# A decoder layer on one core: the weighing of the values in one run behind the next block's queries

## The reference, cut to what matters

```
for i in range(6):
    x = attn_layer(shift_tokens(x), Wqkv[i], q_scale[i], k_scale[i], Wo[i]) + x
    x = ffn_layer(shift_tokens(x), ln_g[i], ln_b[i], W1[i], b1[i], W2[i], b2[i]) + x

# attn_layer, 16 heads of 64, windows of 32 queries over 64 keys
q, k, v = split(x @ Wqkv)
q, k = l2norm(q) * qs, l2norm(k) * ksc
q = q * cos * scale + rotate_half(q) * sin * scale      # k with 1 / scale
sim = einsum('bhwie,bhwje->bhwij', q, k_of_two_windows) * 8     # masked
out = einsum('bhwij,bhwje->bhwie', softmax(sim), v_of_two_windows) @ Wo

# ffn_layer
xn = (x - mean) / sqrt(var + 1e-5) * g + b
a, gate = split(xn @ W1 + b1)
out = a * gelu(gate) @ W2 + b2
```

## Time and profile before

| | |
|---|---|
| median of 3 timed runs | 2067.36 us (2065.05 to 2070.86) |
| the profiled execution | 2071.8 us, of which the span from first to last instruction is 2070.0 us |
| TensorE busy | 1947.8 us, 94% of the span |
| VectorE, ScalarE, GpSimd busy | 1449.9 us, 1371.7 us, 1087.3 us |
| mean granted TensorE clock | 0.988; 1.00 in the stretches of the loop quoted below |
| DMA | 128.39 MB in 82214 packets |

### The profile page before, as it was taken

How to read it: one execution, slowest core, us unless ns; L and a number is a source line. 1 busy time by engine, 2 the same in 40 slices (tenths; PEclk the granted TensorE clock), 3 DMA queues, 4 the chain that set the end, 5 groups by cost and what they waited for, 6 DMA issues and landing times.

```text
span 2070.0 us, 75204 instructions
## 1 busy us (share of the span) xinstructions
PE 1947.8 (94%) x32520; PEld 1179.6 (57%) x32520; DVE 1449.9 (70%) x2239; ACT 1371.7 (66%) x2197; POOL 1087.3 (53%) x709
## 2 busy tenths in 40 slices
PE   8989897689999999999999999999999999999987
PEld 5655655355555555555555555565555555555553
DVE  1454545677787778777877777777777787778773
ACT  5565564466777667766776677767766777677763
POOL 1000000497666666666666666666666666666650
PEclk9999998799999999999999999999999999999998
DMA  3000001032223222232222323222332223222220
GB/s 118 2 1 1 2 21 31 22 83 64 63 64 94 74 74 63 64 94 74 73 64 65 82 75 81 74 65 75 85 80 73 65 62 95 74 74 63 64 64 21
DMA packets 82214, 128.39 MB, mean 62 GB/s; under 512 B 17247, under 2 KB 28125, under 8 KB 81885
## 3 DMA queue, kind: packets, MB, share of 16 engines
q1 hardware_dynamic: 81884, 123.59, 23.1%
HBM read 21.81 MB, written 1.05 MB: 11 GB/s over the span
## 4 chain that ended last, share of the span: by engine, by line
PE 73%; ACT 10%; DVE 10%; issue 6%; DMA 0%; ACTq 0%; SPq 0%; DVEq 0%
PE ps L619 13%; PE ps L623 13%; PE ps L645 9%; PE ps L704 7%; PE ps L696 6%; PE ps L689 6%; PE ps L429 4%; PE ps L669 3%; PE ps L628 3%; PE ps L632 2%; DVE work L1287 2%; DVE work L1106 2%; PE ps L525 2%; PE ps L443 1%; ACT work L1000 1%
## 5 line engine op out<-in xcount | busy, mean ns | idle before, releaser
L1457 POOL TENSOR_TENSOR work<-work,RS 128x1024 f32<-128x1024 f32 x192 | 365.6, 1904 | 385.8 <-ACT RS L971 384.7
L1101 DVE TENSOR_TENSOR work<-ps,work 128x512 f32<-128x512 f32 (+1 forms) x288 | 247.9, 861 | 265.7 <-ACT work L1032 228.6
L623 PEld LDWEIGHTS ps<-ident,work 128*128 128x128 f32 x3072 | 344.1, 141 | 118.6 <-issue 90.0
L623 PE MATMUL ps<-ident,work 128*128 128x128 f32 x3072 | 392.8, 275 | 14.6 <-ACT work L1000 11.2
L1476 POOL TENSOR_TENSOR work<-work 128x1024 f32<-128x1024 f32 x96 | 226.0, 2354 | 108.8 <-DVE work L1106 108.8
L1042 ACT ACTIVATE work<-work 128x1024 f32<-128x1024 f32 x96 | 101.6, 1058 | 268.3 <-DVE work L1216 268.3
L1468 POOL TENSOR_TENSOR work<-work 128x1024 f32<-128x1024 f32 x96 | 227.3, 2368 | 52.6 <-DVE work L1106 52.6
L1106 DVE TENSOR_TENSOR work<-ps,work 128x512 f32<-128x512 f32 (+1 forms) x288 | 247.4, 859 | 0.0
L1170 DVE TENSOR_REDUCE SS<-work 128x16 f32<-128x1024 f32 x192 | 231.6, 1206 | 0.0
L696 PEld LDWEIGHTS ps<-work 64*32 64x32 f32 x12288 | 135.0, 105 | 146.0 <-issue 133.3
L619 PE MATMUL ps<-WQ,XS 128*128 128x512 f32 x384 | 189.3, 616 | 8.0 <-issue 4.3
(11 more groups left out here) (185 smaller groups left out, 3094.0 us busy)
## 6 DMA issues: line engine op xcount, KB each, us to landing
work<-work SPq DMA_DIRECT2D x576, 128.0 KB
work<-work SPq DMA_DIRECT2D x336, 64.0 KB
WQ<-in_wqkv SPq DMA_DIRECT2D x6, 512.0 KB, 3.6
WK<-in_wqkv SPq DMA_DIRECT2D x6, 512.0 KB, 4.1
WV<-in_wqkv SPq DMA_DIRECT2D x6, 512.0 KB, 4.2
WO<-in_wo SPq DMA_DIRECT2D x6, 512.0 KB, 3.9
work<-ZR SPq DMA_DIRECT2D x48, 64.0 KB
W<-in_w SPq DMA_DIRECT2D x6, 341.0 KB, 3.5
```

The costliest lines, as they stand in the source:

```text
L623: m = nc.tensor.transpose(flat(R)[:, t * 128:t * 128 + 128], src[:, t * 128:t * 128 + 128], ident[:, :])
L1101: V.tensor_tensor(h16(cos_part[:, j, cols]), h16(src), rotary_tabs[:, at:at + 64].unsqueeze(1).broadcast_to([PARTS, heads_in, 64]), ALU.mu ...
L1457: U.tensor_tensor(h16(qk_norm[:, j, :]), h16(cos_part[:, j, :]), inv_norms[:, j, :].unsqueeze(2).broadcast_to([PARTS, 16, 64]), ALU.mult). ...
```

## The change

On TensorE, the weighing is issued as one run of 64 calls (128 matmuls) behind the next block's queries, instead of 32 calls before and 32 behind them; the queries get the wait for `probs_turned_copied`. In the steps with n = 0, `turn_tokens` moves from in front of the turning of the heads to behind it. On ScalarE, in the steps with n = 0, `inverse` moves ahead of the copy of the turned queries, and `invert_norms(g, 0)` moves behind the squares of the keys. The scores stay in two halves. VectorE, GpSimd and the DMA queue keep their order.

```
@@ TensorE, step @@
-                if f is not None and n == 0:
-                    turn_tokens(f)
                 if d:
                     pe.wait_ge(heads_copied, g - 2)
                     turn(bank_y, heads, 0, 4).then_inc(heads_turned, 1)
                     turn(bank_y, heads, 4, 8).then_inc(heads_turned, 1)
+                if f is not None and n == 0:
+                    turn_tokens(f)
...
-                if c:
-                    if a:
-                        pe.wait_ge(k_sin, 2 * g + 2)
-                    pe.wait_ge(probs_turned_copied, g - 1)
-                    pe.wait_ge(windows_loaded, 160 * (g - 1))
-                    weigh(0, 4)
                 if fo is not None and n == 2:
                     project_out(fo, 2, 3 if fo < FFN_PASSES - 1 else 8)
...
                 if g + 1 < ALL_BLOCKS:
                     if not b:
                         pe.wait_ge(q_sin, g + 1)
+                    if c:
+                        pe.wait_ge(probs_turned_copied, g - 1)
                     queries(g + 1)
                 if c:
-                    weigh(4, 8).then_inc(heads_weighed, 1)
+                    if a:
+                        pe.wait_ge(k_sin, 2 * g + 2)
+                    pe.wait_ge(probs_turned_copied, g - 1)
+                    pe.wait_ge(windows_loaded, 160 * (g - 1))
+                    weigh(0, 8).then_inc(heads_weighed, 1)
@@ ScalarE, step @@
+                if f is not None and n == 0:
+                    inverse(f)
                 if b:
                     act.wait_ge(q_turned, g)
                     A(q_t[:, :, :], turned(bank_z), ACT.Copy).then_inc(q_turned_copied, 1)
...
-                if f is not None and n == 0:
-                    inverse(f)
                 if f is not None and n == 1:
                     nc.scalar.preload_act_table_set(LNEXP)
+                late = f is not None and n == 0
+                if a and not late:
+                    invert_norms(g, 0)
                 if a:
-                    invert_norms(g, 0)
                     for half in range(2):
                         ...
                         A(squares[:, 1, 512 * half:512 * half + 512], bank_y[:, half, :], ACT.Square).then_inc(k_squared, 1)
+                if a and late:
+                    invert_norms(g, 0)
```

## The result

| | before | after |
|---|---|---|
| median | 2069.11 us (6 runs, 2065.05 to 2071.53) | 2054.63 us (6 runs, 2046.67 to 2058.2) |
| the profiled execution | 2071.8 us, span 2070.0 | 2056.84 us, span 2055.1 |

The changed kernel is faster: the ratio is 0.9925, with an interval of 0.991 to 0.9939. It gains 14.5 us. Forecast were 27.4 us and 2040; 2054.6 lies inside the range of 2024 to 2057, near its upper end.

What follows compares the result with a forecast made beforehand. VectorE's stream was taken to bound the key projection of n = 3 to L628 of n = 1, TensorE the rest. 13 + 8.4 + 1 + 3 + 2 = 27.4 us gave 2040 on the timed scale, range 2024 to 2057.

Steps and rivals of the forecast that it cites:

- Who bounds what: Loop pass: VectorE bounds from n = 3's key projection to n = 1's L628, TensorE elsewhere; pass 66.5 instead of 67.6 us.
- The rival that TensorE bounds throughout: Whole loop: all TensorE's waits and switches count, 41 us gained, 2026 us, a pass of 65.7; chance 0.09.
- `inverse` ahead of the copy: ScalarE, n = 0: VectorE's idle time before L1150 falls from 0.62 to at most 0.1 us; 13 us gained.
- The joined weighing: TensorE, weighing: one small-to-full switch fewer, 0.19 us a step, paying in n = 1 and 2; 8.4 us, bounds 0 and 10.6.
- The tokens behind the heads: TensorE, n = 0: ScalarE's heads copy up to 0.45 us sooner, 11.2 us of waits shrink to a fourth; worth 0.
- What is late next: TensorE: 0.5 to 0.8 us turn up as longer waits at L628 for gating, or partly L689 for the queries' copy.
- The supply of instructions: TensorE's instruction packets: 3 us gained in early steps, net 0 in the loop (-5 to +10), plus 2 from new slack.
- the early steps: TensorE, g = 2 to 5: the wait for VectorE's key products goes and pays only there, about 1 us.
- the gap stays: VectorE before L1150: it waits as before or another wait replaces the 0.62 us; 14 us gained, 2053; chance 0.13.
- Starvation: TensorE, end of the 128 matmuls: packets ending there cost up to 2.3 us each, 2095 us; chance 0.06.

Runs made afterwards that it cites:

- experiment 10: The changed kernel with never-waiting semaphore tests added on TensorE, making a loop pass 2560 instructions, ten packets: 2034.62 us, ratio 0.984 to the kernel before.
- experiment 2: The kernel before with ScalarE's two moves alone (`inverse` ahead of the queries' copy, query norms behind the key squares): 2065.78 us, ratio 0.9984.
- experiment 9: The kernel before with joined weighing and ScalarE's two moves, token transposes still ahead of the heads', padded to 2560 instructions a pass: 2036.99 us, ratio 0.9845.
- padded and joined: The kernel before with the joined weighing alone, padded with never-waiting tests to 2560 instructions a pass: 2043.92 us, ratio 0.9879 to the kernel before.
- experiment 7: The kernel before with only never-waiting semaphore tests added on TensorE, 2560 instructions a pass: 2062.06 us, ratio 0.9964 to the unpadded kernel before.
- experiment 4: The changed kernel with 43 never-waiting tests at the start and 42 a pass (2560 instructions), packet ends held at good places: 2039.4 us, ratio 0.986.
- experiment 5: The same padded changed kernel as experiment 4, with 128 more never-waiting tests at the start, moving packet ends half a packet: 2082.98 us, ratio 1.0071.

## Why the prediction was right and wrong

**Who bounds what: right.** Between the key projection of n = 3 and L628 of n = 1 VectorE's stream is the bound, elsewhere TensorE's. The shortest pass is 66.52 us against 66.5 forecast. With the packets held still (experiment 10) the passes are 66.2 and 66.6 in turn, 66.45 in the mean. The rival that TensorE bounds throughout would have had 65.7.

**`inverse` ahead of the copy: the mechanism right, the size half.** 13 us were counted, 6.9 were measured on top of the joined weighing and some 3 alone, there with more packet stalls than before. The gap did close as forecast, but the 13.9 us were read wrongly. The last of the 23 waits, at the end of the loop, is 3.57 us alone; it only shrinks to 2.7 in experiments 2 and 9. The 22 others are 10.3 us, and most are not 0.62 but 0.62 and 0.2 in turn. The pass before the one of the earlier trace rows has

```profile
1397.81 1.36 DVE L1150 TENSOR_SCALAR YC<-ps,YM,YQ 128x128 f32<-128x128 f32 x4 [0.19 <-ACT YQ L955]
```

And part of the gap is closed by the joined weighing too: the 22 waits are 9.1 us in the padded kernel before, and 5.8 padded and joined. The two terms overlapped and were added.

**The joined weighing: right place, half the size.** 8.4 us were counted, 0.19 a step in two steps of each pass. Measured are 0.17 (1.58 to 1.41) in the run and 0.19 in the queries, 0.36 a step; the steps' shortest times fell by 0.36 in n = 1, from 19.70 to 19.34, and by as much in n = 2 and 3. With 2 x 22 steps that is 15.8 us, and the early steps g = 2 to 8 give 2.8 more in the padded pair (93.9 to 91.1): 18.6, against 18.1 measured. (The median pass of the padded pair falls by 0.68, from 67.56 to 66.88, for twice 0.36.) The upper bound of 10.6 was too low, since it had only one side of the switch. The Trainium skill (TensorEngine Tiling (Array Packing), Key Properties) says that a change of tiling mode drains TensorE and gives no price; here going to small tiles and back costs 0.36 us.

**The tokens behind the heads: right.** It was counted at 0. The medians of the padded runs differ by 2.4 us, the undisturbed passes by 0.01. Its waits at L1000 went as forecast.

**What is late next: right.** L628 was to wait 12 us or more and waits 14.6 (26.4 with the packets still), and the copy of the queries costs 8.7 us at L689.

**The supply of instructions: this is the step that failed.** It counted a gain of 3 us in the early steps and 2 in the loop, +5. Without it the forecast was 22.4 us, and the work itself is worth 27.4 (experiments 7 and 10). What was measured is 14.5, so this term is -12.9 where +5 was counted. The gaps at packet boundaries, added up from the traces, put it at -10.9 in the loop (12.0 to 22.9), beyond the forecast's lower end of -5 there, and at +1.4 in the early steps (5.1 to 3.7), -9.5 together; the rest of the difference is not placed. Three things in it were wrong. It took the packet's least distance, 3.9 us, for a constant, whereas a packet that falls due while the window loads are issued starts up to 7.7 us after the boundary before instead of about 1.0, and the stall at 648.37 ends 9.3 us behind that boundary. It looked for the danger at the end of the long run of weighing, where the trace shows next to nothing (1.5 us at L696 in the whole run), while the stalls stand mostly in the second half of the scores, 14.3 of the 22.9 us in steps n = 0. And it counted ends by old stalls instead of by instruction number: 2518 to a pass and 256 to a packet would have told which passes are hit. That part of it which read the stalls as packets was right. By the rule of the Trainium skill (Runtime: NRT & Kernel Launch, Instruction fetch mechanics), by which the fetch is mostly hidden, the loops of experiments 4 and 5 should have agreed; their 21 passes are 24.8 us apart.

**The rivals.** The measured 2054.6 is next to the 2053 of "the gap stays", and it would be wrong to read it so: the gap went (1.0 us in one wait). Equal times do not show equal causes; the waits do. Starvation came, but elsewhere, and at 12.9 us it took nearly half of the gain and did not turn the result. That the padded kernels give 27.4 us, the very sum that was forecast, is chance: ScalarE's moves gave 6.9 for 13, the joined weighing 18.1 for 8.4 and the 1 us of the early steps, and the 5 of the supply were not in it. That 2054.6 lies in the range owes as much to these errors, which partly cancel, as to the mechanism.

What stays open: why a packet starts late while loads are issued, and how much of that is the number of loads; and how the joined weighing closes part of VectorE's gap.

## What to carry to other kernels

When TensorE stands in the middle of a run of equal matmuls with no semaphore behind it, count its instructions: if the stalls agree modulo 256, the time lost belongs to the place and not to the edit, and two orders can only be compared after padding both so that a loop pass is a multiple of 256. Put the padding where the engine waits anyway, and count its own price: here 0.108 us an instruction where nothing covers it. Count a switch between small and full matmuls on both sides, and do not add up two terms that close the same gap.

## What was not expected of the hardware

- The phase of the packets alone moves the loop's 21 passes from 1404.4 to 1429.2 us, with the same instructions in each (experiments 4 and 5).
- Tests of a semaphore that is long set are not free. An instruction with two of them takes 0.108 us: 128 more at the start of experiment 5 bring the first matmul at 19.45 us instead of 5.71.
- Behind full matmuls that are still being worked off most of that is hidden. In experiment 5 the 20 test instructions in n = 1 lengthen the step's shortest time from 19.34 to 19.76 us, and in experiment 4 the 22 in n = 3 lengthen that step from 16.48 to 16.94; the 13 in n = 3 of experiment 10 leave it at 16.47. Ahead of a wait that TensorE has anyway they cost nothing that shows: the padded kernel before has a shortest pass of 67.56 us against 67.50.
- A packet that falls due while SyncE issues ten loads mostly starts behind them, and hardly sooner when the loads have an eighth of the bytes: 6.0 instead of 6.7 us after the boundary before, at the stall of 1.75 us that becomes 0.96.
